# The order of VectorE's work in attention: two turnings in a row, an addition ahead of two reciprocals, and a reciprocal ahead in the last step

## The reference

```python
x = x + 0.5 * ffn(layernorm(x))      # gelu(h @ w1 + b1) @ w2 + b2, 1024 hidden
x = x + attn(layernorm(x))
x = x + 0.5 * ffn(layernorm(x))      # the same weights

def attn(x):                          # 16 heads of 64
    q, k, v = split(x @ w_qkv)        # q scaled by 64 ** -0.5
    sim = q @ k.T - |i - j| * slope[h]
    sim = where(causal, -max, sim)    # j > i is masked
    return concat(softmax(sim) @ v) @ w_out + b_out
```

## Time and profile before

| | |
|---|---|
| median of 3 runs | 2341.64 us |
| profiled execution, its own time | 2344.32 us |
| its span, first to last instruction | 2342.2 us |
| busy: PE, its weight loads | 2191.1 us (94%), 1776.6 (76%) |
| busy: DVE | 1552.3 us (66%) |
| busy: ACT | 1208.7 us (52%) |
| busy: POOL | 1052.2 us (45%) |
| mean granted TensorE clock | 0.978 of full |

### The profile page before, as it was taken

One profiled execution on the slowest core, in us unless ns is written; L12 is line 12 of the kernel. 1 busy time (PEld: TensorE's weight loads), 2 busy tenths in 40 slices (PEclk: granted clock), 3 DMA queues, 4 the chain that ended last, 5 costly groups with the idle time before them and its releaser, 6 DMA issues.

```text
span 2342.2 us, 41791 instructions
## 1 busy us (share of the span) xinstructions
PE 2191.1 (94%) x14720; PEld 1776.6 (76%) x14720; DVE 1552.3 (66%) x4070; ACT 1208.7 (52%) x3032; POOL 1052.2 (45%) x1770
## 2 busy tenths in 40 slices
PE   6899999999999999999999999999999999999987
PEld 5587787877878778787777878778787787877856
DVE  5675757667667676776757676576666767767563
ACT  4645636455363654736456364554636547364552
POOL 1543626436263453625537164362634536255260
PEclk9999999999999999999999999999999999999998
DMA  3332404224051340514314042240513405143150
GB/s 122 106 85 58 129 14 133 67 70 129 5 146 50 86 113 24 145 32 109 91 52 126 22 131 68 69 130 6 147 48 87 113 26 140 34 108 91 42 144 14
DMA packets 109936, 193.90 MB, mean 83 GB/s; under 512 B 34464, under 2 KB 53152, under 8 KB 109728
## 3 DMA queue, kind: packets, MB, share of 16 engines
q1 hardware_dynamic: 89248, 138.77, 21.1%
q0 software_dynamic: 20480, 52.47, 9.2%
HBM read 14.95 MB, written 8.39 MB: 10 GB/s over the span
## 4 chain that ended last, share of the span: by engine, by line
PE 54%; DVE 22%; POOL 9%; ACT 6%; SPq 5%; issue 3%; DMA 2%; POOLq 0%; DVEq 0%; ACTq 0%
PE ps L269 52%; DVE P L711 10%; POOL P L856 5%; DVE P L703 5%; SPq L219 5%; POOL PT L219 4%; ACT P L548 3%; DVE gl L636 3%; DVE gh L682 2%; DMA PT<-P 2%; PE ps L323 2%; ACT L548 1%; DVE xtl L636 1%; ACT v L515 0%; ACT qk L515 0%
## 5 line engine op out<-in xcount | busy, mean ns | idle before, releaser
L856 POOL TENSOR_SCALAR P<-P,rs 128x512 f32<-128x512 f32 (+3 forms) x1024 | 535.0, 539 | 474.3 <-DVE rs L694 470.9
L548 ACT ACTIVATE P<-P,mx 128x512 f32<-128x512 f32 (+3 forms) x1024 | 563.0, 552 | 239.5 <-DVE mx L703 238.9
L219 POOL DMA_DIRECT2D PT<-P x640 | 323.9, 511 | 350.9 <-DVE P L711 334.4
L711 DVE STREAM_TRANSPOSE P<-P 128x1792 f32<-128x1792 f32 (+1 forms) x256 | 385.0, 1504 | 64.2 <-POOL P L856 64.1
L269 PE MATMUL ps<-PT,v 128*64 128x256 f32 (+1 forms) x3072 | 323.4, 362 | 62.9 <-DMA PT<-P 60.4
L269 PE MATMUL ps<-qk 64*128 64x512 f32 (+3 forms) x2048 | 323.8, 446 | 36.5 <-DVE x L665 27.1
L269 PEld LDWEIGHTS ps<-PT,v 128*64 128x64 f32 x3072 | 222.4, 142 | 159.3 <-issue 81.3
L269 PE MATMUL ps<-w2h,gh 128*128 128x256 f32 x1024 | 302.3, 295 | 16.4 <-DVE gl L636 9.9
L269 PE MATMUL ps<-w2l,gh 128*128 128x256 f32 x1024 | 295.0, 288 | 0.0
L269 PE MATMUL ps<-w2h,gl 128*128 128x256 f32 x1024 | 294.4, 288 | 0.0
L269 PEld LDWEIGHTS ps<-qk 64*128 64x128 f32 x2048 | 171.8, 188 | 157.5 <-issue 76.9
(11 more groups left out here) (74 smaller groups left out, 4413.2 us busy)
## 6 DMA issues: line engine op xcount, KB each, us to landing
PT<-P SPq DMA_DIRECT2D x1408, 80.0 KB, 2.5
PT<-P POOLq DMA_DIRECT2D x640, 80.0 KB, 2.6
x<-in_L_attn_x SPq DMA_DIRECT2D x16, 512.0 KB, 3.9
out_y<-x SPq DMA_DIRECT2D x16, 512.0 KB, 2.9
raw<-in_L_ffn_w SPq DMA_DIRECT2D x2, 512.0 KB, 5.9
raw<-in_L_ffn_w SPq DMA_DIRECT2D x1, 1024.0 KB, 8.8
rawq<-in_L_attn_w_qkv SPq DMA_DIRECT2D x1, 1024.0 KB, 7.3
rawk<-in_L_attn_w_qkv SPq DMA_DIRECT2D x1, 1024.0 KB, 9.4
```

What stands on the lines that cost most here:

```text
L219: e.dma_start(PT[c % 2][32 * m:32 * m + 32, g, :], P[c % 3][32 * g:32 * g + 32, m, :]).then_inc(landed[c % 3].sem, 16)
L548: e.activation(p, p, ACT.Exp, bias=mx[:, r, i:i + 1], scale=-1.0, accum_out=sm[:, r, i:i + 1]).then_inc(s_ex.sem, 1)
L711: e.transpose(p, p).then_inc(s_tr.sem, 1)
L856: e.tensor_scalar(p, p, rs[:, 2 * (c % 2) + h, i:i + 1], 1.0, ALU.mult, ALU.mult).then_inc(s_nz.sem, 1)
```

## The change

Only DVE's order changes; no instruction is added or removed, and no other engine's program.

In `begin`, the addition of down tile 0 goes ahead of the two reciprocals. The pairs 3 and 2 of step 1 go ahead of the second reciprocal and of the large turning. The addition of down tile 1 goes between the two turnings, and the small turning ahead of pairs 0 and 1. In every later step the small turning follows the large one at once, and `biased(b, c, 2)` comes after both. In the last step of a batch with a successor, the reciprocal of pair 6's half 0 goes ahead of the two `ln_lo` and of `biased(b, 7, 3)`.

```diff
@@ begin(b)
-                inverse(b, 0, 1)
-                inverse(b, 0, 0)
                 if b > 0:
                     add3(b - 1, 0)
+                inverse(b, 0, 1)
+                biased(b, 1, 3)
+                biased(b, 1, 2)
+                inverse(b, 0, 0)
                 turned(b, 0, 1)
-                biased(b, 1, 3)
-                turned(b, 0, 0)
-                biased(b, 1, 2)
                 if b > 0:
                     add3(b - 1, 1)
+                turned(b, 0, 0)
                 biased(b, 1, 0)
                 biased(b, 1, 1)
@@ attention(b)
                 for c in range(2, NC):
                     if more and c == NC - 1:
+                        inverse(b, c - 1, 0)
                         ln_lo(1, b + 1, 0)
                         ln_lo(1, b + 1, 1)
-                    biased(b, c, 3)
-                    inverse(b, c - 1, 0)
+                        biased(b, c, 3)
+                    else:
+                        biased(b, c, 3)
+                        inverse(b, c - 1, 0)
                     turned(b, c - 1, 1)
+                    turned(b, c - 1, 0)
                     biased(b, c, 2)
-                    turned(b, c - 1, 0)
                     biased(b, c, 0)
                     biased(b, c, 1)
                     inverse(b, c, 1)
```

## The result

The changed kernel takes 2275.84 us (median of 4 runs, 2270.62 to 2279.03) against 2342.34 us (4 runs, 2340.11 to 2344.06). The ratio is 0.9714, 95% interval 0.9693 to 0.9736: 2.9% faster, forecast 2268. Its profiled execution took 2274.3 us, span 2272.1, which is 70.1 less than the span before.

A forecast was written before the change was run, and what follows sets the result against it. The prediction took PE to pace the kernel, held by waits for spreading DMAs and DVE's additions. Terms 27.1 + 6.2 + 10.8 + 13 + 15 + 3.5 = 75.6 us off 2344.3 gave 2268.7, predicted as 2268; range 2250 to 2300.

The forecast's parts named there:

- Start of a batch: PE's waits for DVE's additions, and the half clock behind them, go in batches with a predecessor: 44.1 us.
- The three terms: Start of a batch: 27.1 us wait at the scores, 6.2 at `dn 2` in seven batches, 10.8 clock in eight.
- the 0.4 of room: Start of a batch: `add3(b-1, 1)` would end 0.4 us before PE wants it for `dn 2`.
- the signs of being right: Listed trace signs, among them PE's waits for the addition falling from 33.3 us to under 3.
- Steps: Middle steps: both turnings in a row remove most of PE's waits for spreading DMAs: 13 us, bounds 3 and 16.
- The ring: Middle steps: a loop through DVE and POOL of 9.4 us, not PE's 9.04, paces each step; 8.5 without the pair.
- The small turning's room of 0.15: Middle steps: POOL's small normalisations are ready 0.15 us before the large turning ends, so the small turning does not wait.
- Last step: End of batches with a successor: wait at `values(b, 6)` falls from 2.26 to 1.24, splits end earlier: 15 us.
- Rival B: Batch end: the cast, 0.45 later, meets POOL's normalisations; 0.6 a batch, 9 us lost: 2277; chance 0.12.
- part 3: Last step's new order, turnings of pair 6 in a row and reciprocal ahead: 1.0 us in each of 15 batches.
- rival D: PE's clock falls to 1.2 GHz as often, at the scores or elsewhere: 10.8 us lost, 2279; chance 0.08.
- Rival E: Steps: later `biased(c, 2)` delays exponentials, so reciprocals wait, 0.97 in six steps of 16 batches: slower, 2393; chance 0.04.

The follow-up runs named there:

- experiment 5: Kernel before with only a batch's first addition moved ahead of the two reciprocals: 2359.31 us against 2340.64, ratio 1.0090.
- experiment 2: Kernel before with only the two turnings in a row in steps 2 to 6: 2325.57 us against 2344.73, ratio 0.9918.
- experiment 3: Kernel before with only the last step's new order (reciprocal ahead, turnings in a row, last pair behind): 2339.62 us against 2344.73, ratio 0.9990.
- experiment 4: Changed kernel without its last-step order (`begin` and steps 2 to 6 new): 2272.94 us against 2344.73 for the kernel before, ratio 0.9699.
- experiment 8: Changed kernel with POOL's bias of the next batch one step earlier: 2241.40 us against 2340.64 for the kernel before, ratio 0.9575.
- experiment 9: Changed kernel with POOL's bias one step earlier and pair 7's large turning ahead of the first gelu split: 2234.27 us; ratio to the kernel before 0.9545.
- experiment 11: Changed kernel with pair 7's large turning ahead of the first gelu split, bias where it was: 2267.72 us; ratio to the kernel before 0.9671.
- experiment 10: Changed kernel without its last-step order, with POOL's bias one step earlier: 2253.16 us against 2340.64 for the kernel before, ratio 0.9624.
- experiment 7: Changed kernel with the last step's reciprocal back in its old place behind the pair: 2266.05 us against 2344.69 for the kernel before, ratio 0.9658.
- experiment 1: Kernel before with only the new order in `begin`, every later step as before: 2290.37 us against 2344.73, ratio 0.9769.
- experiment 6: Kernel before with both additions moved as in the change, pairs and turnings in the old order: 2299.98 us against 2344.69, ratio 0.9809.

## Why the prediction was right, and where not

- **Start of a batch: 44.1 forecast, 48.7 measured** (45.3 in batches 1 to 14 and 3.4 in the last). Right in the sum, wrong in the split: I booked 27.1 us to the first addition alone, and experiment 5 shows that alone it loses 19. The three terms are one gain that needs both additions. And PE came to `dn 2` sooner than I reckoned: 1031.01 - 1024.12 = 6.89 after the first scores, for my 1066.98 - 1059.41 = 7.57. The pair of score matmuls behind a wait had cost 0.7 beside the wait, which I counted as work: the next matmul came 1064.24 - 1059.41 - 1.78 = 3.05 after the first scores, and in the unbroken row it comes 1026.48 - 1024.12 = 2.36 after them. The addition itself ends 7.16 after the scores, just as reckoned. So the 0.4 of room was a wait of 0.29, and PE's waits for the addition fell to 4.8, not to under 3 as the signs of being right had it.
- **Batch 0: 2.6 forecast, 2.7 measured.**
- **Steps: 13 forecast (3 to 16), 20.6 measured** (19.7 and 0.9), above my bound. The ring was right (9.4 reckoned, turnings 9.60 apart measured, experiment 2); the size was off. I took only idle time that the timeline marks. Batch 7 shows one wait of 0.64 in its middle steps and took 48.61 against 47.70 with no wait; batch 3, with the wait of 2.51 and a half clock after it, took 52.01 against 48.40.
- **The small turning's room of 0.15 held.** Turnings wait for POOL 20 times where they did 86 times, and only 3 of these are between S2 and S7.
- **Last batch's end: 0.9 forecast, 1.3 measured** (1.0 up to V6 and 0.3 behind it).
- **Last step: 15 forecast, -4.6 measured** (15.4 at `values(b, 6)`, and -20.0 behind). The wait there is 1.07 to 1.26 in all 15 batches, forecast 1.24. The step that failed is "the first split has the large turning between it and the held cast, 0.45 fits". It fits in the nine good batches, which are 0.9 shorter from S7 to S0'. But POOL's run starts 1.0 earlier against the scores and the first cast later by just about 0.45 (2.20 ahead of where `values(b, 6)` would start without its wait, for 2.64). So the cast comes 2.47 into the run in place of 1.00, where POOL passes from one normalisation to the next, and in four batches it is shut out until the end of the bias. Rival B had this mechanism with a price of 0.6 in every batch; it is 3.6 to 4.6 in four batches, clock included, and 1.5 in two more that show a half clock but no long cast. Experiments 3 and 4 show part 3 as the cause of the long casts, and experiments 8, 9 and 11 that moving the bias or the cast ends them. Nor did the forecast gain come about where the bias was out of the way: experiments 8 and 10 differ by 0.1 in ten batches, and by 1.6 to 1.8 in five, through the clock behind the wait at `values(b, 6)`, which the forecast left out.
- **The clock** stays at 2.4 GHz after the first scores in the 15 batches with a predecessor, as forecast, but rival D was in part right: it falls elsewhere, behind the gelu waits of six batches. Before it fell at seven batch ends, where it cost nothing.
- **Rival E** did not come about: reciprocals wait 48 times, none of them in steps 2 to 6. The 15 waits in step 7 are those of the moved reciprocal (experiment 7).

Between the profiled executions the sum was 75.6 and the change 70.1. Start (+4.6), steps (+7.6), batch 0 and the last batch's end (+0.5) and 1.4 of chance at the beginning stand against -19.6 in the last step. That the total came so close is luck: the last step alone is off by 19.6, and the other terms cancel most of it.

## What to carry to other kernels

When two waits of one engine hang on one other engine's order, price them together: freeing the first alone can merge them into one longer stop, and the long stop can cost the clock as well. In a ring over three engines count the ring's length beside the busiest engine's step; an instruction taken out of the ring pays until the two are equal. Before a cast on DVE is shifted by half a microsecond, look at what POOL runs back to back at that time, and put POOL's movable work where it waits anyway. And when a part yields about what was forecast, look at it batch by batch: experiment 10 has the right size from another cause.

## What the runs showed of the hardware

- A cast on DVE that meets a run of back-to-back POOL instructions can be held until the next hand-over between two of them or for the whole run: 0.79 and 4.21 us at the same 2.47 us offset. At an offset of 2.46 to 2.48, the hand-over from the fourth to the fifth normalisation, 12 of 45 were held for the whole run (changed kernel, experiments 3 and 7); at 1.00, inside the second, none of 105 (before, experiments 1, 2, 4, 5, 6 and 10), and none took over 1.80. A cast that arrives during the last instruction of the run, the bias, takes 2.21 or 2.22, until 0.29 after its end (15 of 15 in experiment 11). The rule of the Trainium skill cited ahead (SBUF — State Buffer, "Who interferes with whom") has whoever issues first keep the other off for its whole instruction. The trace agrees where one instruction is waited for; the 12 casts that waited for four normalisations and the bias it does not explain.
- Short stops were followed by a half clock in an engine that is busy otherwise. Behind stops of 1.78 us (one of 2.15) PE ran at 1.2 GHz in 8 of 15 batches before; behind stops of 2.1 to 2.3 us at `values(b, 6)` in 7 of 15 before and in 5 of 15 in experiment 10; behind 3.35 us in 13 of batches 1 to 14 of experiment 5. With no stop over 1.3 us from batch 1 to batch 14 (experiment 9) the mean granted clock there is 1.00, by this window:

```profile
200.00:2170.00 1970.00, 1930.12 (x13342) 1563.85 (x13342) 1361.57 (x3682) 1081.53 (x2768) 961.53 (x1642) 1.00 0.33 88
```
